# A two-layer graph convolution on Trainium2: no absolute value in the softplus, window columns copied by ScalarE, and a one-hot built with a second operand from PSUM

## What is computed

```python
def _cgconv(x, src, dst, edge_attr, Wf, bf, Ws, bs, gamma, beta, rmean, rvar):
    z = jnp.concatenate([x[dst], x[src], edge_attr], axis=-1)
    msg = jax.nn.sigmoid(z @ Wf + bf) * jax.nn.softplus(z @ Ws + bs)
    n = x.shape[0]
    summed = jax.ops.segment_sum(msg, dst, num_segments=n)
    cnt = jax.ops.segment_sum(jnp.ones((dst.shape[0],), x.dtype), dst, num_segments=n)
    out = summed / jnp.maximum(cnt, 1.0)[:, None]
    out = (out - rmean) * jax.lax.rsqrt(rvar + BN_EPS) * gamma + beta
    return out + x
...
x = _layernorm(x + two_layers(x, ...), axis=-1)
```

## Time and profile before

| | |
|---|---|
| time, median of 3 runs | 2848.38 us (2832.99 to 2863.74) |
| span of the profiled execution | 2110.8 us |
| difference of the two | 737.6 us |
| busy in the profile: DVE, ACT, PE, POOL | 1801.2, 1677.5, 1557.2, 1515.1 us |
| slots, and gathers of 128 rows | 392 and 1568 |

### The profile page before, as it was taken

The page is one execution under the profiler, slowest core; times in us unless marked ns, Lnnn a source line. Parts: engine busy times, 40 slices in busy tenths (PEclk is TensorE's granted clock), DMA queues, the critical chain, the costliest instruction groups (busy, mean ns, idle before and its releaser), DMA issues. The chain is left out here.

```text
span 2110.8 us, 35689 instructions
## 1 busy us (share of the span) xinstructions
PE 1557.2 (74%) x8321; PEld 1286.2 (61%) x8321; DVE 1801.2 (85%) x4354; ACT 1677.5 (79%) x2908; POOL 1515.1 (72%) x1589
## 2 busy tenths in 40 slices
PE   7777767767767787677487777777676776877773
PEld 6666656656556666566376666666565665665652
DVE  6899989989889898898549999898898887988887
ACT  5798888878878788788467888888787887887884
POOL 6677777777777777777267777777777777777770
PEclk9999999999999899999799999999999998999995
DMA  8455555555555555555475555555555555555542
GB/s 291 138 156 166 156 166 155 163 158 156 158 160 156 155 156 165 152 157 155 147 224 156 154 166 165 156 163 156 156 158 161 155 155 156 162 157 156 154 143 62
DMA packets 161806, 336.71 MB, mean 160 GB/s; under 512 B 58866, under 2 KB 85610, under 8 KB 161671
## 3 DMA queue, kind: packets, MB, share of 16 engines
q0 software_dynamic: 74496, 202.13, 32.5%
q1 hardware_dynamic: 85654, 131.58, 20.4%
q10 hardware_dynamic: 1522, 1.72, 0.3%
HBM read 315.49 MB, written 19.81 MB: 159 GB/s over the span
## 5 line engine op out<-in xcount | busy, mean ns | idle before, releaser
L344 POOL DMA_INDIRECT pre<-s_rows,ends x1512 | 1451.3, 960 | 473.8 <-issue 448.1
L458 PE MATMUL pre_ps<-rhs,lhs 128*128 128x256 f32 x3136 | 854.8, 417 | 463.5 <-DVE lhs L696 462.1
L458 PEld LDWEIGHTS pre_ps<-rhs,lhs 128*128 128x128 f32 x3136 | 607.0, 204 | 676.1 <-DVE lhs L696 385.0
L716 DVE TENSOR_TENSOR pre<-pre_ps,pre 128x1024 f32<-128x1024 f32 x378 | 460.7, 1219 | 52.6 <-DMA pre<-s_rows,ends 51.1
L548 ACT ACTIVATE pre<-pre 128x512 f32<-128x512 f32 x392 | 246.9, 630 | 309.3 <-DVE pre L716 270.0
L471 PEld LDWEIGHTS sum_ps<-hot,msg 128*128 128x128 f32 x3136 | 441.6, 204 | 53.2 <-issue 15.5
L696 DVE TENSOR_SCALAR lhs<-lhs,base_f,part 64x256 f32<-64x256 int32 x784 | 340.9, 435 | 114.2 <-issue 106.5
L471 PE MATMUL sum_ps<-hot,msg 128*128 128x64 f32 x3136 | 418.1, 279 | 24.8 <-DVE sums L736 24.8
L553 ACT ACTIVATE logs<-pre 128x1024 f32<-128x1024 f32 x392 | 414.3, 1057 | 12.4
L543 ACT COPY rhs<-dst_ps 64x256 f32<-64x256 f32 x792 | 290.0, 366 | 24.8 <-PE dst_ps L445 6.6
L727 DVE TENSOR_TENSOR msg<-soft_ps,logs 128x512 f32<-128x512 f32 x392 | 271.0, 691 | 13.6
(11 more groups left out here) (88 smaller groups left out, 570.8 us busy)
## 6 DMA issues: line engine op xcount, KB each, us to landing
lhs<-dge_and_destination_cols SPq DMA_DIRECT2D x196, 512.0 KB
pre<-s_rows,ends POOLq DMA_INDIRECT x1512
s_rows<-logs SPq DMA_DIRECT2D x8, 512.0 KB, 7.1
s_rows<-x_t SPq DMA_DIRECT2D x7, 512.0 KB, 10.8
s_rows<-msg SPq DMA_DIRECT2D x6, 512.0 KB, 6.1
x_rows<-pre SPq DMA_DIRECT2D x12, 256.0 KB, 4.5
out<-y_out SPq DMA_DIRECT2D x12, 256.0 KB, 2.3
ends<-edge_ends SPq DMA_DIRECT2D x100, 16.0 KB, 3.6
```

The lines of the kernel that those rows point to most:

```text
L344: nc.gpsimd.indirect_dma_start(pre[:, slot(k, j), i, 0:width], None, rows, bass.IndirectOffsetOnAxis(ap=ends[:, k, j * TILES + i, 0:1], ax ...
L458: ins = nc.tensor.matmul(pre_ps[:, j % 2, i, :], lhs[:, j // 2, edges], rhs[:, j, i // 2, :], start=True, stop=not plain(b, k, j))
L716: nc.vector.tensor_tensor(rows, pre_ps[:, j % 2], rows, ALU.add).then_inc(s_pre[j], 1)
```

## The change

Three edits, in both layers.

1. The absolute value and its third of `pre` go. ACT makes exp(-f) and exp(s) in two instructions of 512 columns, and the softplus becomes max(min(log(1 + exp(s)), 40), s), so that an overflow of exp is cut off. `pre` has 256 columns a tile where it had 384.
2. `window_cols` moves from DVE to ACT, between `rows` and `exponents`, and the register loads for it with it (`next_bases`).
3. `hot_transposed` becomes a `scalar_tensor_tensor`: (destination - base) == part, with `part` read as a broadcast tensor from the unused columns of the PSUM bank of `sum_ps`, where it is written once in each layer. Because PE writes this bank in `window_sum`, DVE now waits for the window sum of slot n-4 ahead of `hot_transposed` of n, where it waited ahead of `add_up`, behind it. On PE the first window sum waits for the fourth one-hot.

```diff
-        pre = sb("pre", [P, RING, TILES, 3 * F], F32)
+        pre = sb("pre", [P, RING, TILES, F2], F32)
...
+        part_ps = sum_ps[:, 0, 0, WIN:WIN + PAIRS]
...
             def window_sum(g, j):
                 done(pe, s_msg, g, j, 0)
                 done(pe, s_hot, g, j, 0)
+                if isinstance(g, int) and g == 0 and j == 0:
+                    pe.wait_ge(s_hot_t[3], 1)
                 done(pe, s_added, g, j, 1)
...
-            def absolute(g, j, at):
+            def exponents(g, j, at):
                 done(act, s_pre, g, j, 0)
-                nc.scalar.activation(pre[:, at, :, F2:3 * F], pre[:, at, :, F:F2], ACT.Abs).then_inc(s_abs[j], 1)
-
-            def exponents(g, j, at):
-                done(act, s_abs, g, j, 0)
                 done(act, s_msg, g, j, 2)
-                nc.scalar.activation(logs[:, j % 2].rearrange("p k (h f) -> p k h f", f=F),
-                                     pre[:, at].rearrange("p k (h f) -> p k h f", f=F)[:, :, 0:3:2, :],
-                                     ACT.Exp, scale=-1.0).then_inc(s_expo[j], 1)
+                nc.scalar.activation(logs[:, j % 2, :, 0:F], pre[:, at, :, 0:F], ACT.Exp, scale=-1.0)
+                nc.scalar.activation(logs[:, j % 2, :, F:F2], pre[:, at, :, F:F2], ACT.Exp).then_inc(s_expo[j], 1)
...
+            def window_cols(g, j, at):
+                done(act, s_dst, g, j, 0)
+                for q in range(PAIRS):
+                    ins = nc.scalar.copy(x_cols[:, j, q, :], x[:, bass.ds(at[PAIRS * j + q], WIN)])
+                ins.then_inc(s_cols[j], 1)
...
             def one(b, k):
                 g = group_no(b, k)
+                cols_at = next_bases(b, k)
                 for j in range(SLOTS):
                     rows(*ahead(g, j))
-                    absolute(g, j, slot(k, j))
+                    window_cols(g, j, cols_at)
                     exponents(g, j, slot(k, j))
...
-                    ins = nc.vector.tensor_scalar(lhs[hot_rows[q], j // 2, at],
-                                                  lhs[hot_rows[q], j // 2, at].bitcast(I32),
-                                                  base_f[hot_rows[q], k, PAIRS * j + q:PAIRS * j + q + 1],
-                                                  t["part"][hot_rows[q], q:q + 1], ALU.subtract, ALU.is_equal)
+                    ins = nc.vector.scalar_tensor_tensor(lhs[hot_rows[q], j // 2, at],
+                                                         lhs[hot_rows[q], j // 2, at].bitcast(I32),
+                                                         base_f[hot_rows[q], k, PAIRS * j + q:PAIRS * j + q + 1],
+                                                         part_ps[hot_rows[q], q:q + 1].to_broadcast([WIN, PAIR]),
+                                                         ALU.subtract, ALU.is_equal)
...
-                nc.vector.scalar_tensor_tensor(soft_ps[:, j % 2], pre[:, at, :, F:F2], 0.0, soft_ps[:, j % 2],
-                                               ALU.max, ALU.add).then_inc(s_soft[j], 1)
+                nc.vector.scalar_tensor_tensor(soft_ps[:, j % 2], soft_ps[:, j % 2], SOFT_TOP, pre[:, at, :, F:F2],
+                                               ALU.min, ALU.max).then_inc(s_soft[j], 1)
...
+                if four_back:
+                    done(v, s_sum, four_back[0], four_back[2], 0)
                 if live(0):
                     hot_transposed(b, k, j)
...
                     add_up(four_back[0], four_back[2], 0, sum_at)
-                if live(0):
-                    window_cols(g, j, 0, cols_at)
-                if four_back:
                     add_up(four_back[0], four_back[2], 1, sum_at)
-                if live(0):
-                    window_cols(g, j, 1, cols_at)
```

More of the change, by code:

```diff
@@ L23 @@
 LN_EPS = 1e-5
+SOFT_TOP = 40.0
 WIN = 64
@@ L96, in graph_layer @@
         s_stage = [logs[:, 0], logs[:, 1], rows_of(msg[:, 0:2]), rows_of(msg[:, 2:4]), rows_of(hot[:])]
-        row_stage = [pre[:, w // 3, :, w % 3 * F:(w % 3 + 1) * F] for w in range(QUADS)]
+        row_stage = [pre[:].rearrange("p r k f -> p (r k f)")[:, w * 4 * F:(w + 1) * 4 * F]
+                     .rearrange("p (k f) -> p k f", f=F) for w in range(QUADS)]
         if first:
@@ L119, in graph_layer @@
         s_base, s_rel = sem("base_done"), sem("rel_done")
-        s_hot_t, s_prod, s_pre, s_abs = each("hot_t_done"), each("prod_done"), each("pre_done"), each("abs_done")
+        s_hot_t, s_prod, s_pre = each("hot_t_done"), each("prod_done"), each("pre_done")
         s_expo, s_log_f, s_log_s = each("expo_done"), each("log_f_done"), each("log_s_done")
@@ L566, in gate, with next_bases @@
                                      ).then_inc(s_gate[j], 1)
+            def window_cols(g, j, at):
[3 more added lines that the diff above has]
+                ins.then_inc(s_cols[j], 1)
+            def next_bases(b, k):
+                turn = (b if isinstance(b, int) else b + 1) if k < BODY - 1 else (1 if isinstance(b, int) else b + 2)
+                act.wait_ge(base_in[(k + 1) % BODY], turn * 16 + 16 if isinstance(turn, int) else turn * 16)
+                act.sem_inc(passed, 1)
+                return nc.values_load_multi_w_load_instructions(
+                    base_i[0:1, (k + 1) % BODY, :], engines=[ENG.Activation], min_val=0, max_val=NPAD - WIN,
+                    skip_runtime_bounds_check_because="every entry of the table is clamped")[1]
             def one(b, k):
                 g = group_no(b, k)
+                cols_at = next_bases(b, k)
                 for j in range(SLOTS):
                     rows(*ahead(g, j))
-                    absolute(g, j, slot(k, j))
+                    window_cols(g, j, cols_at)
                     exponents(g, j, slot(k, j))
@@ L590, in _ @@
                     act.wait_ge(x_in[c], 16)
+            else:
+                act.wait_ge(x_ready, CHUNKS)
             turns(act, bodies, one)
@@ L624, in _ @@
                 after(nc.vector.tensor_tensor(flag[:, 1:2], flag[:, 0:1], sum_ps[0:1, 0, 0, 0:1], ALU.add))
+                v.wait_ge(iotas, 3)
+                after(nc.vector.tensor_copy(part_ps, t["part"][:]))
                 after(nc.vector.tensor_scalar(flag[:, 2:3], flag[:, 1:2], 1.0, None, ALU.min))
@@ L657, in _ @@
                 v.sem_inc(planned, 1)
+                nc.vector.tensor_copy(part_ps, t["part"][:]).then_inc(scaled, 1)
+                v.wait_ge(scaled, 1)
                 v.wait_ge(cnt_in, 16)
@@ L666, in _ @@
                                             ALU.mult).then_inc(scaled, 1)
-                    v.wait_ge(scaled, c + 1)
+                    v.wait_ge(scaled, c + 2)
                     nc.vector.scalar_tensor_tensor(t["x1_t"][:, cols], t["sums"][:, 0, cols], t["bn_scale"][:, 0:1],
@@ L730, in add_up @@
             def add_up(g, j, q, at):
-                done(v, s_sum, g, j, 0)
                 if q:
@@ L748, in copy_turned, with stages @@
                 nc.vector.tensor_copy(pre[:, m, :, F:F2], turn_ps[m % 2]).then_inc(x_copied, 1)
[L750 to L757, removed]
+            def stages(b, k, j, sum_at, live=lambda lag: True):
                 g = group_no(b, k)
@@ L812, in one @@
                     sum_at = load_bases((k - 1) % BODY)
[L813 to L817, removed]
                 for j in range(SLOTS):
@@ L823, in one @@
                             prepare(b, 0, 1 if isinstance(b, int) else b + 2)
-                    stages(b, k, j, sum_at, cols_at)
+                    stages(b, k, j, sum_at)
             if first:
@@ L839, in _ @@
             for j in range(SLOTS):
-                stages(bodies, 0, j, sum_at, None, lambda lag, j=j: j < lag)
+                stages(bodies, 0, j, sum_at, lambda lag, j=j: j < lag)
             for j in range(SLOTS):
```

## The result

| | before | after |
|---|---|---|
| time, median (least to greatest), 10 runs each | 2847.12 us (2832.99 to 2863.74) | 2859.61 us (2855.17 to 2873.59) |
| ratio, with its 95% interval | | 1.005 (1.0033 to 1.0068), that is +12.5 us |
| span of the profiled execution | 2110.8 us, clock 0.925 | 2871.8 us, clock 0.806 |

The change is 0.5% slower, where the forecast was 20 us faster. One thing has to be said for these numbers to be read: the trace ahead of the prediction isn't a trace of what was timed. In the experiments five chips ran the kernel before in 2831 to 2867 us (one run more took 2909 us); a sixth ran it in 2117.60 to 2123.07 us, in all of its seven runs. By its span and its clock the first trace is of the second kind: the seven runs have spans of 2116 to 2121 us and granted clocks of 0.916 to 0.921.

A forecast was written before the change was run, and what follows sets the result against it. POOL's starting of gathers was taken as the bound, VectorE nearly even with 51.1 us in hand. Gathers -22, ends -2 and VectorE lateness +4 gave -20 us: 2848 to 2828 us, range 2605 to 2880.

The forecast's parts named there:

- POOL spends 1984 us of 2110.8 on starting gathers: POOL's 1568 gathers, 0.960 us each plus a 0.305 us gap, were taken to set the pace: 5.06 us a slot.
- The sum is made against the span, and its difference is set against the median as it is: Savings reckoned on the 2110.8 us span were applied unchanged to the 2848.38 us median, leaving 737.6 us between them unexplained.
- The first rival: Gathers and VectorE's one-hots and copies exclude each other in timed runs: up to 486 us faster, 2362 us; chance 0.24.
- The closing test: The reckoning would be wrong if the time moved over 60 us while the profile's span moved by 20.
- VectorE's copies and register loads: Taking window copies off VectorE saves 0.1 us a slot; half its register loads, some 29 us, go too.
- The moved wait: VectorE's earlier wait for the window sum, ahead of the one-hot: 71 us at most, 45 taken, on 59 lower-clock slots.
- the slower case: VectorE becomes the bound through the moved wait, up to 1.2 us per touched slot; 2920 us at 145 slots; chance 0.16.
- its threshold of 85 slots: Touched slots at which the moved wait uses up VectorE's 51 us in hand, 29 from register loads and POOL's 22.
- Gathers, -22 us: POOL's gathers shorten from mean 960 to median 946 ns as VectorE's edited instructions stop hindering them: 22 us less.
- The one-hot, 0.479 us: VectorE's new one-hot of 256 columns takes 479 ns where it took 435: about 0.09 to 0.10 us more a slot.
- ACT, +0.01 us a slot: ACT saves 0.43 us on exponentials and absolute value, pays 0.44 for two copies; at worst +0.30, covered by 0.69 of waiting.
- The 2 us of the layers' ends: The chain from sums to softplus shortens by 0.43 us, counting only in a layer's three last slots: 1 us each.

The follow-up runs named there:

- before again: Nothing changed: the kernel before was run and traced once more, to get a trace of its timed kind; 2847.61 us.
- wait alone: Kernel before with only the moved wait of the third edit, the one-hot staying a tensor_scalar with both operands in SBUF; 2887.11 us, ratio 1.0163.
- edit 3 alone: Kernel before with only the one-hot's operand in PSUM and the moved wait; 2890.46 us, ratio 1.0158.
- the runs with the pause: A GpSimd memset of 128x1024, waited for, ahead of each slot's four gathers: kernel before 2694.32 us, changed kernel 2643.26 us, on different chips.
- edit 1 alone: Kernel before with only the absolute value removed; 2846.14 us, ratio 0.9998.
- the last run: Changed kernel with all three edits and a GpSimd memset ahead of each slot's gathers; 2643.26 us, on the chip running the kernel before in 2120 us.

## Why the prediction failed, step by step

**"POOL spends 1984 us of 2110.8 on starting gathers": the failed step.** It was read correctly from the earlier trace rows, and it was the pace of that execution alone. In the timed runs GpSimd waits 742.2 us (before) and 696.2 us (after) for the softplus, and VectorE's chain behind each stop sets the time. "The sum is made against the span, and its difference is set against the median as it is" carried the error on: an unread 35% was treated as a constant, though some 660 us of it hang on this very loop. The first rival named that risk and chose the wrong mechanism: the gathers are hardly longer in the timed runs (mean 971 ns before again, 972 after, against 960 in the earlier trace rows). The closing test, that the reckoning is wrong if the time moves by more than 60 us while the span moves by 20, missed it; the sign was that the span after was 2871.8 us.

**VectorE's copies and register loads: mechanism right, credit wrong.** They were counted as 0.1 us a slot and 29 us of register loads, 68 us in all. The loads were given to slack and the copies set against the longer one-hot. Together they were worth 25 us of time: VectorE has no slack there, and what is missing to 68 went, as far as the traces tell, into longer stops.

**The moved wait: size right by luck, price wrong.** I took 45 us and set it against 29 + 51 us in hand. It measured 42 to 46 us (wait alone, edit 3 alone), paid in full. That the size agrees is luck, as the 45 us were reckoned from slots at the lower clock and the 42 to 46 us come with the stops. Each stop finds the one-hot undone, so the product follows it (1016.10 us above), the window sum follows the product, and the next one-hot waits for that. The view of waits has 111 such waits in 170.1 us; the text had said that at over 100 us the slower case has come. That rival, which had a chance of 0.16, is the one whose direction came true, but its threshold of 85 slots had no part in it: VectorE's chain behind the stops was the bound before the change already. Edit 2 gave back more than half of the 43 us.

**Gathers, -22 us: worth nothing in the timed runs.** 971 and 972 ns, with 259 and 253 gathers of over 1 us. A faster gather is also worth nothing to an engine that waits 700 us. Where GpSimd is the pace the forecast's mechanism has something for it: in the runs with the pause the mean is 960 ns in the kernel before and 951 ns in the changed one, near the 946 to 950 foretold, which over 1568 gathers makes an estimated 14 us. These two runs are from different chips, so this is a hint and not a comparison. What lengthens these 250 gathers of the timed runs, most of them to 1.09 us, isn't known; the change left it as it was.

The rule of the Trainium skill, page "SBUF — State Buffer", section "Who interferes with whom", by which GpSimd and VectorE's copies and `tensor_scalar` in two-port modes lock each other out, agrees with the runs with the pause: beside the memset of the pause VectorE's copies took 635 ns in place of 212 and its `tensor_scalar` 671 in place of 449 (kernel before again), while the `scalar_tensor_tensor` of the last run took 486 in place of 479.

**The one-hot, 0.479 us: right. ACT, +0.01 us a slot: the parts right, the sum a little too high.** 479 ns; exponentials of 629 and 613 ns, copies of 242 ns where I took 0.22. ACT's busy time fell by 62 us (1677.4 to 1615.5), 0.16 us a slot, since the absolute value took 0.54 us a slot with it (edit 1 alone) and not 0.43. None of it counts: edit 1 alone is level. The 2 us of the layers' ends are below what was measured.

## What to carry to other kernels

Where a trace's span and the timed runs differ by a third, the trace may be, as here, of another kind of execution. Its bound, its slack and what they cover say nothing of the time until a trace of the timed kind is there, and the range has to be made as if all slack were zero. A wait on TensorE's signal that is moved ahead of work that others need can cost even where it is hardly ever late in the first trace: when the signal comes late, all that stands behind it is late too. And an engine that waits is worth a test with less to do, or with a pause: here a memset of 0.97 us in a slot, useless in itself, took off 5.5%.

## What the runs showed of the hardware

- With four gathers a slot, each 1.25 us behind the last, half of TensorE's signals came over 1 us late in the kernel before again (574 of 1149), 307 of them over 5 us, and several were recorded within a few tenths of a microsecond. Five of six chips run this kernel in the time that goes with that. With half the gathers it was 1%, with a pause in each slot 4%. With half the bytes or a shorter run ahead it stayed at half, and with less work on TensorE VectorE's waits for "remote" stayed near their size (645.7 and 685.9 us). Why signals of TensorE are held up by gathers, how long an unbroken run of them it takes, and why one chip shows none, is open.
- The stops have a rhythm: the ends of VectorE's gaps lie 20.6 us apart in the median in the kernel before, three slots, and 27.4 us after, four slots. What sets it wasn't found.
- Whether the change without the pause is faster or slower on a chip without stops wasn't tried.
